# Four layers of attention on one core: full-width value steps behind both pairs of scores, the ones for the keys written a batch ahead, and no GpSimd additions in the first layer's last unit

## What is computed

```python
tokens = x.reshape(B, C, N).transpose(0, 2, 1)
qkv = (tokens @ w_proj + b_proj).reshape(B, N, NUM_HEADS, 3 * HEAD_DIM)
q, k, v = jnp.split(qkv, 3, axis=-1)
attn = jnp.einsum('bihd,bjhd->bijh', q, k) * SCALE
attn = jax.nn.softmax(attn, axis=2)
res = jnp.einsum('bijh,bjhd->bihd', attn, v).reshape(B, N, NUM_HEADS * HEAD_DIM)
out = res @ w_out + b_out + tokens
```

## Time and profile before

| | us |
|---|---|
| median of 3 timed runs | 3213.33 (3209.35 to 3216.2) |
| span of the profiled execution | 3214.9 |
| TensorE (PE) busy | 2731.7 (85%) |
| VectorE (DVE) busy | 2212.3 (69%) |
| ScalarE (ACT) busy | 1234.2 (38%) |
| GpSimd (POOL) busy | 657.1 (20%) |
| maxima of score tiles on VectorE (L871) | 512 of 1219 ns |
| exponentials of the first layer (L660) | 512 of 1023 ns |
| additions into `acc0`: GpSimd (L547), VectorE (L903) | 208 and 96 |

### The profile page before, as it was taken

The page is one execution under the profiler, slowest core; times in us unless marked ns, Lnnn a source line. Parts: engine busy times, 40 slices in busy tenths (PEclk is TensorE's granted clock), DMA queues, the critical chain, the costliest instruction groups (busy, mean ns, idle before and its releaser), DMA issues.

```text
span 3214.9 us, 45307 instructions
## 1 busy us (share of the span) xinstructions
PE 2731.7 (85%) x16502; PEld 1884.4 (59%) x16502; DVE 2212.3 (69%) x2474; ACT 1234.2 (38%) x1348; POOL 657.1 (20%) x397
## 2 busy tenths in 40 slices
PE   5889969899798897988879888798887998878983
PEld 4447754577545774457744677447764477644772
DVE  4766668666686675866668666785677756777666
ACT  2443325433254332543335333353333533244333
POOL 0430115201061021500225002340024300243011
PEclk8989989999899998999989999899988999889996
DMA  6100050000500004000040000400022000310015
GB/s 152 23 24 1 1 120 6 24 1 14 113 1 24 1 14 113 1 24 1 14 112 1 24 1 32 95 1 24 1 64 62 24 1 1 92 35 24 1 53 235
DMA packets 46400, 124.77 MB, mean 39 GB/s; under 512 B 9792, under 2 KB 21312, under 8 KB 42560
## 3 DMA queue, kind: packets, MB, share of 16 engines
q1 hardware_dynamic: 46144, 121.41, 14.1%
HBM read 43.01 MB, written 23.86 MB: 21 GB/s over the span
## 4 chain that ended last, share of the span: by engine, by line
PE 65%; DVE 12%; issue 9%; SPq 4%; DMA 4%; ACT 4%; DVEq 0%; ACTq 0%
PE tile L1264 22%; PE pv L1264 10%; PE tile L1358 8%; PE pv L1374 6%; PE tile L1336 5%; DVE small L871 4%; PE tile L1518 4%; SPq L445 4%; PE tile L1395 3%; DMA stack<-ones 2%; PE tile L1540 2%; PE tile L1648 1%; PE tile L1567 1%; PE tile L1417 1%; DMA stack<-qk_r 1%
## 5 line engine op out<-in xcount | busy, mean ns | idle before, releaser
L871 DVE TENSOR_REDUCE small<-tile 128x1 f32<-128x1024 f32 x512 | 610.6, 1219 | 210.9 <-PE tile L1336 210.1
L660 ACT ACTIVATE p<-tile 128x1024 f32<-128x1024 f32 x512 | 520.9, 1023 | 568.9 <-PE tile L1358 564.5
L1358 PE MATMUL tile<-stack 112*128 112x512 f32 x1024 | 387.0, 462 | 129.5 <-DMA stack<-ones 87.8
L547 POOL TENSOR_TENSOR acc<-acc,p 128x1024 f32<-128x1024 f32 x160 | 397.6, 2505 | 176.9 <-DVE acc L903 175.0
L1264 PE MATMUL tile<-qk_r 128*128 128x512 f32 x1536 | 378.0, 395 | 0.0
L1336 PE MATMUL tile<-stack 96*128 96x512 f32 x1024 | 339.8, 424 | 34.9 <-DMA stack<-qk_r 31.0
L1358 PEld LDWEIGHTS tile<-stack 112*128 112x128 f32 x1024 | 162.9, 196 | 350.7 <-issue 227.5
L572 POOL TENSOR_TENSOR row_sum<-act 128x256 f32<-128x256 f32 x32 | 42.1, 1335 | 1488.9 <-DVE act L1099 1488.9
L1374 PE MATMUL pv<-p,v 128*32 128x256 f32 (+1 forms) x3584 | 321.2, 431 | 9.4 <-ACT p L660 7.6
L1264 PEld LDWEIGHTS tile<-qk_r 128*128 128x128 f32 x1536 | 287.1, 188 | 66.6 <-issue 7.7
L1104 DVE TENSOR_TENSOR pl<-p,ph 128x1024 fp32r<-128x1024 f32 x128 | 158.2, 1236 | 238.2 <-ACT p L745 238.2
(11 more groups left out here) (277 smaller groups left out, 4356.9 us busy)
## 6 DMA issues: line engine op xcount, KB each, us to landing
stack<-qk_r SPq DMA_DIRECT2D x192, 256.0 KB, 5.0
x_in<-in_x_dram SPq DMA_DIRECT2D x9, 1024.0 KB, 7.6
act<-in_x_dram SPq DMA_DIRECT2D x8, 1024.0 KB, 11.0
x_scratch<-act SPq DMA_DIRECT2D x7, 1024.0 KB, 3.9
z_scratch<-zbuf SPq DMA_DIRECT2D x7, 1024.0 KB, 5.1
stack<-ones SPq DMA_DIRECT2D x8, 512.0 KB, 10.1
w3f<-w3f_scratch SPq DMA_DIRECT2D x8, 512.0 KB, 3.3
fin_rest<-z_scratch SPq DMA_DIRECT2D x3, 1024.0 KB, 12.6
```

Of the source, the lines that this page charges most:

```text
L547: pe.tensor_tensor(total, first, p0[:, jt % DEPTH, pair, :], ALU.add).then_inc(pool_done, gps.one("add0", *u, jt, pair))
L660: sc.activation(p0[:, jt % DEPTH, pair, :], tile_wait(b, "st0", *u, jt, pair), ACT.Exp, scale=float(D) ** -0.5).then_inc(scalar_done, scal ...
L871: ve.tensor_reduce(maxima[:, h * NT + it:h * NT + it + 1], t[:], X, ALU.max).then_inc(vector_done, vector.one("max0", g, h, it))
L1358: ins = mm(o[:, halves[k]], stack[0:K0, 1, g, h, jt * P:(jt + 1) * P], stack[0:K0, 0, g, h, halves[half]], start=True, stop=True)
```

## The change

Three things. (1) TensorE: per key tile both pairs' scores (st0, s0, st0, s0) and then the whole value step of the key tile before, 512 wide, where two halves of 256 stood between them. (2) SyncE: the ones are copied once in the set-up and then, in each batch but the last, after TensorE's step "g", for the batch that follows. (3) In the last unit VectorE does all ten additions, where GpSimd did two, and x1(0) stands before the additions of its place instead of behind them.

```diff
     if (g, half) == UNITS[-1]:
-        return "pool" if pair == 0 and jt % 2 == 0 else "vector"
+        return "vector"
...
+            s += [("x1", 0, ct) for ct in range(CT)] if u == UNITS[-1] and jt == 5 else []
             for pair in range(2):
                 s += [("max0", *rows_of(following, 2 * jt + pair))] if following else []
                 s += [("add0", *u, jt - 1, pair)] if jt and adder(*u, jt - 1, pair) == "vector" else []
             s += [("res_lo", *last)] if last and jt == 3 else []
-            s += [("x1", 0, ct) for ct in range(CT)] if u == UNITS[-1] and jt == 5 else []
...
+            def key_ones():
+
+                sp.dma_start(stack[IMAX:K0, 1].rearrange("p g h (a n) -> p (g h a) n", n=P).bitcast(F32),
+                             ones[0:NMAX, :].rearrange("p (a n) -> p a n", a=1)
+                             .broadcast_to((NMAX, NG * G * N // P, P))).then_inc(key_ones_in, 16)
+
+            sp.wait_ge(vector_done, vector.count)
+            key_ones()
...
-                sp.dma_start(stack[IMAX:K0, 1].rearrange("p g h (a n) -> p (g h a) n", n=P).bitcast(F32),
-                             ones[0:NMAX, :].rearrange("p (a n) -> p a n", a=1)
-                             .broadcast_to((NMAX, NG * G * N // P, P))).then_inc(key_ones_in, 16)
...
                 sp.dma_start(x3_dram[b], act[:]).then_inc(x3_stored, 16)
+                sp.wait_ge(tensor_done, tensor.at(b, "g"))
+                key_ones()
                 sp.wait_ge(scalar_done, scalar.at(b, "z_kept", CT - 1))
...
+                def pv0(g, half, jt):
+
+                    scalar_wait("exp0", g, half, jt, 1)
+                    if jt == 0 and g == 1:
+                        scalar_wait("pv0_out", 0, half)
+                    for h in range(G):
+                        ins = mm(pv[D * h:D * h + D, halves[half]], v0[:, jt, g * P + D * h:g * P + D * h + D],
+                                 p0[:, jt % DEPTH, h // 2, halves[h % 2]], start=jt == 0, stop=jt == NT - 1)
+                    ins.then_inc(tensor_done, tensor.one("pv0", g, half, jt))
...
                             st0(*u, jt, pair)
                             if following:
                                 s0(*rows_of(following, 2 * jt + pair))
-                            if jt:
-                                pv0(*u, jt - 1, pair)
+                        if jt:
+                            pv0(*u, jt - 1)
```

## The result

| | median us | range us | runs |
|---|---|---|---|
| before | 3211.34 | 3207.17 to 3216.2 | 4 |
| after | 3100.16 | 3092.33 to 3102.0 | 4 |

The ratio of after to before is 0.9639, with a 95% interval from 0.9618 to 0.966 (taken over the rounds of both kernels; the medians' quotient, 0.9654, lies within it). The forecast was 3105, its own range 3090 to 3120. The profiled execution of after has a span of 3100.0 us, where that of before had 3214.9: 114.9 less.

What follows compares the result with a forecast made beforehand. Bound: a chain of waits through TensorE's tiles, VectorE's row maxima and SyncE's stack and ones copies. 56 + 36 + 16 = 108 us off the 3214.9 span gives 3106.9, forecast 3105; own range 3090 to 3120 (50%), 3082 to 3138 for 8 in 10.

Steps and rivals of the forecast that it cites:

- Part 1: Batch start: ones copied earlier, first exponential 7.0 us sooner, last stack copy landing between 4.7 and 6.7; 56 us, 42 to 64.
- The 0.2 us for the low clock: First unit's start: taken off each batch because the next tiles still run at TensorE's lower clock; at most 0.9 us.
- R2: Batch start: last stack copy stays slow behind the input load and low clock costs 0.9; total 3119 or 3135 us; 27%.
- Part 2: Last unit: x1's wait 1.55, full width 1.3 and 0.3, clock 1.3, together 4.45 a batch; 36 us, between 20 and 42.
- (c): Last unit: full-width values cut a key tile from 2.47 to near 2.26 us; 1.3 over six, plus 0.3 in key tile 1.
- step d): Last unit: the clock's fall behind the 1.55 us wait for x1 goes with that wait; 1.3 us a batch.
- Step a): Last unit: GpSimd's two additions go to VectorE, where one takes 1.21 us without GpSimd beside it, 3.29 with it.
- the room before den0: Last unit: VectorE's four additions behind x1 end at 603.4, den0 would start at 604.1; 0.7 us of room.
- Part 3: Three other units: key tile stays 3.40 us, slow VectorE waits shrink, 0.65 a unit; 16 us, between -12 and +30.
- R1: First layer's units: the new wait in each key tile lowers the clock; up to 500 us, at half 3355 us; 3%.
- R3: Other units: the three tile buffers bind harder than, nothing absorbed, their gain -12; total 3133 us; 13%.
- R4: More gained than forecast: 64 us from the ones and 30 from the other units; total 3083 us; 7%.

Runs made afterwards that it cites:

- e1: The kernel before with only the ones' copy moved a batch ahead; 3147.87 us, ratio 0.9792.
- e3: The kernel before with only the value steps at full width behind both pairs; 3207.12 us, ratio 0.9981.
- e4: The changed kernel with the value steps in halves again; 3142.09 us, ratio 0.9781.
- e6: The changed kernel with two of the last unit's additions on GpSimd again, x1 still ahead; 3099.25 us, ratio 0.9632.
- e8: The changed kernel with exponentials over half of each tile in the second and third unit, output not the reference's; 3094.7 us, ratio 0.9635.
- e2: The kernel before with all ten last-unit additions on VectorE and x1 ahead of its additions, values still in halves; 3198.31 us, ratio 0.9957.
- e5: The changed kernel with x1(0) behind the two additions again, all ten additions still on VectorE; 3128.23 us, ratio 0.9737.
- e7: The changed kernel with the full value step between the two pairs in the three units with row maxima; 3123.14 us, ratio 0.9709.
- e10: The changed kernel with five tiny ScalarE operations ahead of the second layer's square root, which also moved its table load; 3120.16 us, ratio 0.9702.
- e11: The changed kernel with ten tiny ScalarE operations ahead of the second layer's square root, which also moved its table load; 3119.41 us, ratio 0.9704.
- e9: The changed kernel with VectorE's low half of res one key tile later in the second and third unit; 3101.87 us, ratio 0.9643.

## Why the prediction was right, point by point

**Part 1, the ones: 56 predicted, 62 measured.** The copy cost nothing in its new place, as argued. The middle that I took between a stack copy's 4.7 and 6.7 us was too high by most of its half: the last copy lands in 4.7, though the input load stands right behind it. It was the ones that had slowed it, as e1 shows by moving them alone. The prediction read the ring order of the Trainium skill (DMA: Bandwidth & Descriptors, "Queues, rings and completion order") as saying that a transfer behind the copy doesn't delay it, which gave 64. That reading holds in this case where the input load follows the copy (4.7), and not where the ones do (6.7). The 0.2 us for the low clock is neither of the two measured prices. With half values it costs 0.52 (e1). With full ones the first unit is 28.85 against 28.91 in e3, so nothing, but not because the clock rises sooner: the exponential of key tile 2 still comes 0.45 later behind the first one than in e3 (7.59 against 7.14, means). e3 loses this lead at key tile 6, where TensorE waits for VectorE (0.65 us in the second batch) and the changed kernel doesn't. R2 (the copy stays slow) is out.

**Part 2, the last unit: 36 predicted, 41.5 measured.** The stage table takes it apart, as 32.53 (before), 31.20 (e1), 29.59 (e4), 27.34 (after). x1's wait: 1.61 against 1.55. Full width: 2.25 against 1.6 (c), since a key tile takes 2.12 and not 2.26. The prediction's own terms, 2.47 less 0.15 and 0.1, give 2.22, so a part of this is a slip in its sum; and the price for a change between tile and value step was too small, 0.1 where 2.47 - 2.12 - 0.15 leaves 0.20. The clock: 1.33 against 1.3, but step d) failed in its cause. I let the fall go with the wait; e1 keeps the wait and loses the fall. Step a) is right about the price and wrong about its place in the sum: e6 shows that it may be left out. And the room before den0, put at 0.7, is gone: the four additions end at 573.45 + 4.62 = 578.07, den0 starts at 578.13 and its weight load has waited 0.76 for them. In all eight batches it is 0.05 or 0.06 behind them. So one of the prediction's own signs of being wrong, den0 waiting for VectorE, did come, at a price of about 0.04 a batch (den0 at 4.59 behind x1's end, 4.55 in e6). x1 starts at 572.13 only because out0 ends then; the additions are already the next bound, beside TensorE.

**Part 3, the other units: 16 predicted, 9 measured.** All the named waits are there: 0.17 to 0.19 for the exponential in most key tiles (0.14 by hand), 0.39 and 0.50 behind the slow VectorE step of the second and third unit (0.5), and the transposes at the unit's end wait no more. The term that failed is the steady key tile: 3.40 by hand, 3.50 in the trace. The fourth tile comes at 1.84 as reckoned, but from there to the value step it is 0.66 (504.15 to 504.81), not 0.56: behind the wait the tile itself takes 0.73, where the same tile without a wait takes 0.65 in e8 and the value step comes 0.58 behind it. Over six key tiles that 0.10 eats what the slow step and the unit's end gave back, and the second and third unit gain only 0.13 and 0.12. The first unit gains 0.83 (6.7 us in all), though not at its start, where the low clock puts it 0.41 behind (key tile 2, 7.59 against 7.18 behind the first exponential, means): it gains 0.34 in the next key tile, 0.84 from key tile 5 to 6, behind VectorE's slow addition, and 0.33 from key tile 7 on. The prediction had named 3.5 as the sign of being wrong, and for this part it was; the range for it, -12 to +30, held.

**Rivals.** R1, the clock: the second and third unit run at full clock in all eight batches in spite of the waits in them (stretches of the second unit and of the last up to den0, granted clock third from the end):

```profile
488.00:521.40 33.40, 31.78 (x236) 15.12 (x233) 28.90 (x30) 17.45 (x19) 19.14 (x8) 1.00 0.00 1
...
554.70:578.13 23.43, 23.17 (x203) 11.80 (x200) 18.29 (x21) 15.61 (x18) 0.00 (x0) 1.00 0.01 1
```

The Trainium skill's rule of "psum-queue depth-cycling" (TensorE: Matmul & The Clock Gate) isn't borne out at these waits of 0.18 to 0.5 us. R3 was half right: the buffers bind harder than by hand, by 0.10 in each key tile where it had 0.15 in three of eight, but the slow step is absorbed, which it denied. R4 was half right too (part 1 near 64, part 3 not).

**The sum.** 108 predicted, 114.9 in the spans: +6 and +5.5 in the first two parts, -7 in the third, +2.6 in the rests that no step had. That the total came within 5 us is in part luck: the errors cancel. The parts alone give 68.9, 19.2 and 8.7 in the spans (e1 to e3), 97 together, 18 less than the change. Full width in the last unit, worth 0.4 us a batch until x1 is ahead and 2.25 behind that, is the largest interaction, but 1.33 of it is offset, since e1 and e2 both count the clock's fall: the unit leaves 4 us of the 18. Another 4.5 are in the first unit, where e1's loss of 0.52 a batch is covered in the whole change. The other 9 are no work of an edit that a run shows: 3 in the rests and 7 ahead of the first batch's stages and behind the eighth's, stretches that differ as much between kernels with the same code there, less 1 at the batches' starts.

## What to carry to other kernels

A wait with a fixed end hides the worth of every other edit in its stage: in the last unit full width gained 0.4 us a batch alone and 2.25 once x1 was out of the way, so test an edit again after the wait behind it is gone, and test whether the edits that came with it are still needed (e6). When a step is put behind others to cover a wait, price the wait that remains together with the lost overlap behind it, by a row of the trace that has both; here 0.10 us left out in each key tile took most of what two units should have gained. And before a few us are put down to an edit, compare the stages that it doesn't touch.

## What the runs showed of the hardware that was not expected

**The same instructions, three lengths.** The rest of a batch, whose instructions are the same in the changed kernel, e5 and e7, takes 249.0 to 250.0 us in five of the seven of after, 251.47 in one, 255.80 in one; 251.7 to 252.1 in six of e5 and 255.2 in one; 249.0 to 249.8 in all of e7. Busy time by stretch, 187.5 to 212.5 us behind the load of w3f, of a rest of 249.99 us and of the one of 255.80 in the changed kernel:

```profile
393.39:405.89 12.50, 9.48 (x45) 6.59 (x45) 10.77 (x16) 3.50 (x4) 3.60 (x5) 0.91 0.00 0
405.89:418.39 12.50, 10.79 (x48) 9.03 (x47) 6.36 (x14) 4.45 (x7) 0.00 (x0) 0.81 0.35 44
```

```profile
769.37:781.87 12.50, 10.00 (x43) 7.68 (x42) 10.45 (x14) 4.12 (x4) 4.18 (x9) 0.77 0.06 22
781.87:794.37 12.50, 10.13 (x37) 8.73 (x38) 7.49 (x16) 2.94 (x5) 1.40 (x1) 0.50 0.35 43
```

Granted clocks of 0.91 and 0.81, of 0.77 and 0.50 (all of the stretch at the lower level, 1.2 GHz), and of 0.90 and 0.73 for a rest of 251.68 in e5, for nearly the same work. With e1's last unit this fits a clock that falls behind the same stall at some times and not at others. A shift of a few us early in a batch can then go with up to 6 us late in it, and so can a mere difference between batches of one kernel. The four runs of the changed kernel itself, 3092.33 to 3102.0, have mean clocks from 0.938 to 0.935. 12 of e5's 20 us come from there. What decides it stays open: e10 and e11 give one rest for two delays and another pattern of the clock, as T5 would have it. But the table load moved with them, both delays are near to each other, and no run separates the idle time that they add from its place in time.

**One transfer slows its neighbours.** With the ones gone from behind the stack copies, the last of these lands in 4.7 us instead of 6.7 (over the eight batches 4.7 to 5.6 instead of 6.5 to 6.8, in e1 4.6 to 5.1), and the input load right behind it in 8.0 instead of 11.0 (medians of the pages); the ones take 7.6 in their new place instead of 10.1. Whether it is their small pieces (128 values, 512 B) or the one source that they all read that slows the others, no run separates.

**VectorE beside GpSimd.** The same operation, the low half of res, takes 0.75 us with GpSimd idle (last unit of after), 2.52 (after) and 2.94 (e8) with its additions beside it all the time, and 1.48 in e9, where GpSimd's run of additions ends 0.93 us behind the operation's start: what it costs depends on where the additions lie, so moving it (e9) shortened it by 1.04 us and won nothing.
